# Graph network layer pair: 7 of 391 units of 256 edges fetched row by row from SyncE, GpSimd's ring cut from twelve units to ten

## The reference

```python
# layer 1: x = x + attention(relu(layernorm(x)))      (the change leaves it as it is)
# layer 2: h = relu(layernorm(x)); twice:
def _gcn_layer(x, W, b, src, dst, n_nodes):
    h = x @ W
    deg = segment_sum(ones, dst) + 2.0
    dinv = rsqrt(deg)
    msgs = h[src] * (dinv[src] * dinv[dst])[:, None]
    agg = segment_sum(msgs, dst, num_segments=n_nodes)
    return agg + h * (2.0 * dinv * dinv)[:, None] + b
```

## Time and profile before

| | us |
|---|---|
| median of three runs (4146.49 to 4154.21) | 4146.84 |
| profiled execution, span from first to last instruction | 4150.1 |
| first convolution, first to last gather issue | 1943.4 to 2919.7 |
| second convolution, first to last gather issue | 3132.6 to 4114.3 |
| busy: PE, DVE, ACT, POOL | 3489.9, 2288.9, 1798.3, 2607.4 |

### The profile page before, as it was taken

The page is one execution under the profiler, slowest core; times in us unless marked ns, Lnnn a source line. Parts: engine busy times, 40 slices in busy tenths (PEclk is TensorE's granted clock), DMA queues, the critical chain, the costliest instruction groups (busy, mean ns, idle before and its releaser), DMA issues.

```text
span 4150.1 us, 55488 instructions
## 1 busy us (share of the span) xinstructions
PE 3489.9 (84%) x15160; PEld 1694.2 (41%) x15160; DVE 2288.9 (55%) x3880; ACT 1798.3 (43%) x4172; POOL 2607.4 (63%) x2733
## 2 busy tenths in 40 slices
PE   5899988677888888898788888888997788888887
PEld 4499963222233333343333333333443333333332
DVE  6599887677777888885222333333552222333336
ACT  4356522444545555454333443444343333344442
POOL 3654411677777777654777777777106777777775
PEclk9999999899999999999999999999998999999999
DMA  7822325577777777665777777777216777777779
GB/s 285 244 67 61 90 76 208 172 210 210 210 210 211 210 210 211 190 206 190 210 210 210 210 210 210 211 210 210 79 66 211 211 210 210 210 210 210 210 209 351
DMA packets 318375, 804.24 MB, mean 194 GB/s; under 512 B 72905, under 2 KB 98139, under 8 KB 317129
## 3 DMA queue, kind: packets, MB, share of 16 engines
q0 software_dynamic: 199680, 630.72, 52.6%
q1 hardware_dynamic: 88925, 116.91, 8.5%
q10 hardware_dynamic: 29580, 54.49, 3.8%
HBM read 714.52 MB, written 88.21 MB: 193 GB/s over the span
## 4 chain that ended last, share of the span: by engine, by line
PE 34%; POOL 23%; issue 21%; DMA 12%; DVE 6%; SPq 1%; POOLq 1%; DVEq 1%; ACT 1%; ACTq 0%
POOL edge L1280 17%; PE mm L1529 8%; POOL rows_wmat L1280 5%; DMA edge<-h_tab,src_group 5%; DMA rows_wmat<-v_tab,src_group 4%; PE mm L1621 4%; PE sm L1693 4%; PE tr L1621 4%; PE mm L1693 4%; PE sm L1566 3%; PE tr L1693 2%; DVE edge L866 2%; PE tr L1524 1%; DMA ht_tab<-rows_wmat 1%; PE hist_ps L1693 1%
## 5 line engine op out<-in xcount | busy, mean ns | idle before, releaser
L1280 POOL DMA_INDIRECT edge<-h_tab,src_group x1564 | 1484.2, 949 | 708.5 <-issue 447.5
L1436 ACT ACTIVATE hots<-iota,drel 128x128 f32<-128x128 f32 x1760 | 538.0, 388 | 1174.5 <-PE tr L1693 606.9
L1280 POOL DMA_INDIRECT rows_wmat<-v_tab,src_group x782 | 739.4, 945 | 289.2 <-issue 272.4
L1693 PE MATMUL mm<-edge,hots 128*128 x880 | 465.9, 679 | 195.3 <-SPq L1098 189.7
L1693 PE MATMUL sm<-edge,hots 128*128 x880 | 442.6, 650 | 150.5 <-SPq L1098 148.1
L891 DVE TENSOR_TENSOR big<-big,mm 128x512 f32 x220 | 151.4, 688 | 686.6 <-PE tr L1693 668.8
L891 DVE TENSOR_TENSOR big<-big,sm 128x512 f32 x220 | 151.4, 688 | 602.6 <-PE misc L1693 588.6
L1693 PE MATMUL tr<-edge,hots 128*128 x880 | 395.6, 592 | 0.0
L1693 PEld LDWEIGHTS mm<-edge,hots 128*128 128x128 f32 x880 | 183.6, 217 | 470.1 <-issue 469.9
L1529 PE MATMUL mm<-rows_wmat 128*128 128x512 f32 x784 | 356.0, 598 | 0.0
L1693 PEld LDWEIGHTS sm<-edge,hots 128*128 128x128 f32 x880 | 175.8, 207 | 410.3 <-issue 410.0
(11 more groups left out here) (252 smaller groups left out, 4574.0 us busy)
## 6 DMA issues: line engine op xcount, KB each, us to landing
h_tab<-rows_wmat SPq DMA_DIRECT2D x98, 256.0 KB, 2.0
edge<-h_tab,src_group POOLq DMA_INDIRECT x1564, 3.7
rows_wmat<-low_tab SPq DMA_DIRECT2D x157, 128.0 KB
ht_tab<-rows_wmat SPq DMA_DIRECT2D x49, 256.0 KB
big<-ht_tab ACTq DMA_DIRECT2D x49, 256.0 KB, 2.8
v_tab<-rows_wmat ACTq DMA_DIRECT2D x49, 256.0 KB
x_tab<-big SPq DMA_DIRECT2D x49, 256.0 KB, 2.1
rows_wmat<-v_tab,src_group POOLq DMA_INDIRECT x782, 3.7
```

What stands on the lines that cost most here:

```text
L1280: pool.indirect_dma_start(ring[:, 2 * u + c, :], None, tab, bass.IndirectOffsetOnAxis(ap=src_group[:, n:n + 1], axis=0)).then_inc(a["rows_ ...
L1436: act.activation(group_hots[:, q % 2, e, :], iota[:, :], ACT.Abs, bias=drel[:, col:col + 1], scale=-1.0).then_inc(a["dist_set"], 1)
L1693: last = pe.matmul(agg_ps[bank][:, :], group_hots[:, q % 2, w % GROUP * 2 + n, :], edge[:, ds(slot[w % OFFS] + n * D, D)], start=(n == 0), ...
```

## The change

In each of the two convolutions, units 48, 97, 146, 195, 244, 293 and 342 (every 49th) are no longer gathered by GpSimd. SP fetches their 256 rows one by one, with 256 DMAs of 2 KB, whose source address comes from a register. The registers are read from a row of 256 offsets in SBUF, 16 at a time; that row is loaded by one DMA per unit from a new table, `offs_tab` (the sources times 512, made by one DVE operation on 128x782 integers and stored by SP before `low_tab`). These units lie in two slots of their own, at the place of the last two of the twelve; GpSimd's ring has the other ten.

SP does this inside its counting loop: it goes over the 192 pairs of units that GpSimd gathers, in seven rounds of 24 pairs and a last one of 24 without fetches. Ahead of the count of a pair it issues a batch of 16 rows, in two of every three pairs (BATCHES); at the end of a round it waits for the 256 rows and counts the unit. The attention layer keeps its ring of six, and its rows are counted as before. On DVE, the five operations that gave each step's slot in a ring of twelve become seventeen that give it in a ring of ten or in one of the two own slots; the rest of `gather` does the same wait and the same two indirect DMAs per unit.

```diff
-TWELFTH = -(-2 ** 16 // 12)
+EVERY = 49
+OWN = [g for g in range(UNITS) if g % EVERY == EVERY - 1]
+POOLED = [g for g in range(UNITS) if g % EVERY != EVERY - 1]
+POOL_SLOTS = RING[1] - 2
+BATCH = 16
+BATCHES = (1, 1, 0) * 8
...
+        own_offs = eler_hots[0:1, 0:2 * GE].bitcast(I32).rearrange("p (b e) -> p b e", b=2)
...
+            did(dve.tensor_scalar(off_i, src_flat[:, 0:J], float(D), None, ALU.mult))
+            marks["offs"] = prep[0]
...
-            did(dve.tensor_scalar(slotcol_i[1][:, :], gidx[:, :], float(TWELFTH), None, ALU.mult))
...
+            did(dve.tensor_scalar(slotcol_i[1][:, :], gidx[:, :], float(PER_EVERY), None, ALU.mult))
...
             sp.wait_ge(dve_prep, marks["low_T"])
+            sp.dma_start(offs_tab.rearrange("g e -> (g e)").rearrange("(p j) -> p j", j=J), off_i).then_inc(offs_kept, 16)
...
+            def load_offs(k):
+                sp.dma_start(own_offs[:, k % 2, :], offs_tab[OWN[k]:OWN[k] + 1, :]).then_inc(offs_in[k % 2], 16)
+
+            def fetch_and_count_rows(a, tab):
+                again = a["turn"] - 1
+                flat = tab.rearrange("n d -> (n d)")
+                own_before = [again * len(range(b, len(OWN), 2)) for b in range(2)]
+                batch = 0
+                load_offs(0)
+                for i in range(len(POOLED) // 2):
+                    k, at = divmod(i, len(BATCHES))
+                    if k < len(OWN):
+                        b = k % 2
+                        fetched = own_before[b] + k // 2 + 1
+                        if at == 0:
+                            batch = 0
+                            if k + 1 < len(OWN):
+                                load_offs(k + 1)
+                            sp.wait_ge(offs_in[b], 16 * fetched)
+                        for _ in range(BATCHES[at]):
+                            _, offs = nc.values_load_multi_w_load_instructions(
+                                own_offs[:, b, batch * BATCH:(batch + 1) * BATCH], engines=(mybir.EngineType.SP,), min_val=0,
+                                max_val=(NP - 1) * D, skip_runtime_bounds_check_because="rows of the edges' sources")
+                            for n in range(BATCH):
+                                c, p = divmod(batch * BATCH + n, P)
+                                at_slot = 2 * (POOL_SLOTS + b) + c
+                                sp.dma_start(gcn_ring[p:p + 1, at_slot, :], flat[ds(offs[n], D)].rearrange(
+                                    "(a n) -> a n", a=1)).then_inc(own_in[b], 16)
+                            batch += 1
+                    u = i % len(a["rows_in"])
+                    sp.wait_ge(a["rows_in"][u], a["rows_before"][u] + 64 * (i // len(a["rows_in"]) + 1))
+                    sp.sem_inc(a["rows_ready"], 2)
+                    if k < len(OWN) and at == len(BATCHES) - 1:
+                        sp.wait_ge(own_in[b], 16 * GE * fetched)
+                        sp.sem_inc(a["rows_ready"], 1)
...
-            count_rows(agg[1])
+            all_kept(sp, mids[0]["kept"])
+            sp.wait_ge(offs_kept, 16)
+            fetch_and_count_rows(agg[1], h2_tab)
...
-            count_rows(agg[2])
+            fetch_and_count_rows(agg[2], h3_tab)
...
-                for g in range(UNITS):
-                    u, past = g % units, g - units
+                for m, g in enumerate(a["pooled"]):
+                    u = m % units
+                    if m >= units and m % a["told"] == 0:
+                        freed = a["pooled"][m - units + a["told"] - 1]
...
```

More of the change, by code:

```diff
@@ L303, in build @@
         step_of = part(CUT.blocks * P).bitcast(I32)
+        off_i = part(J).bitcast(I32)
         g_from = part(CUT.blocks ** 2 * P // 2).bitcast(BF16).rearrange("p (g n) -> p g n", n=CUT.blocks * P)
@@ L361, in build @@
         ht_kept, low_before = low_in, [16 * len(range(n, TILES, HT)) for n in range(HT)]
-        gcn_rows_in = [sem(f"gcn_rows_in{u}") for u in range(RING[1] // 2)]
+        gcn_rows_in = [sem(f"gcn_rows_in{u}") for u in range(POOL_SLOTS // 2)]
+        own_in = [sem("own_in0"), sem("own_in1")]
+        offs_kept, offs_in = sem("offs_kept"), [sem("offs_in0"), sem("offs_in1")]
         gat_rows_in = [sem(f"gat_rows_in{u}") for u in range(RING[0])]
@@ L365, in build @@
         for n, (name, c) in enumerate((("gat", 0), ("gcn1", 1), ("gcn2", 1))):
-            units = RING[c]
             agg.append(dict(
-                units=units, told=1 + c,
+                units=(RING[0], POOL_SLOTS)[c], told=1 + c, pooled=(range(UNITS), POOLED)[c], turn=n,
                 rows_in=(gat_rows_in, gcn_rows_in)[c],
-                rows_before=[32 * (n == 2) * sum(1 for g in range(UNITS) if g % units // 2 == u) for u in range(units // 2)]
-                if c else [0] * units,
+                rows_before=[64 * (n == 2) * len(range(u, len(POOLED) // 2, POOL_SLOTS // 2)) for u in range(POOL_SLOTS // 2)]
+                if c else [0] * RING[0],
                 rows_ready=sem(f"{name}_rows_ready"),
@@ L658, in _ @@
             did(dve.tensor_scalar(slotcol_i[0][:, :], cols[:, 5, :], -1.0, float(2 * AW), ALU.add, ALU.mult))
[L659 removed]
+            turn_of, is_own, place, own_place = cols[:, 2, :], cols[:, 3, :], cols[:, 4, :], cols[:, 5, :]
+            did(dve.tensor_scalar(slotcol_i[1][:, :], gidx[:, :], float(PER_EVERY), None, ALU.mult))
             did(dve.tensor_scalar(slotcol_i[1][:, :], slotcol_i[1][:, :], 16, None, ALU.arith_shift_right))
[L661 to L663 removed]
+            did(dve.tensor_copy(turn_of, slotcol_i[1][:, :]))
+            issue(dve.scalar_tensor_tensor(is_own, turn_of, -float(EVERY), cols[:, 0, :], ALU.mult, ALU.add))
+            issue(dve.tensor_tensor(place, cols[:, 0, :], turn_of, ALU.subtract))
+            did(dve.tensor_scalar(slotcol_i[1][:, :], slotcol_i[1][:, :], 1, None, ALU.bitwise_and))
+            issue(dve.tensor_scalar(is_own, is_own, float(EVERY), None, ALU.is_ge))
+            did(dve.tensor_copy(own_place, slotcol_i[1][:, :]))
+            issue(dve.tensor_scalar(own_place, own_place, float(POOL_SLOTS + 1), None, ALU.add))
+            did(dve.tensor_scalar(slotcol_i[1][:, :], place, -1.0, float(PER_POOL), ALU.add, ALU.mult))
+            did(dve.tensor_scalar(slotcol_i[1][:, :], slotcol_i[1][:, :], 16, None, ALU.arith_shift_right))
+            did(dve.tensor_copy(turn_of, slotcol_i[1][:, :]))
+            did(dve.scalar_tensor_tensor(place, turn_of, -float(POOL_SLOTS), place, ALU.mult, ALU.add))
+            did(dve.tensor_tensor(own_place, own_place, place, ALU.subtract))
+            did(dve.tensor_tensor(own_place, own_place, is_own, ALU.mult))
+            did(dve.tensor_tensor(place, place, own_place, ALU.add))
+            did(dve.tensor_scalar(slotcol_i[1][:, :], place, -1.0, float(2 * D), ALU.add, ALU.mult))
             did(dve.tensor_tensor(cols[:, 4, :], cols[:, 1, :], stepf[:, 0:blocks], ALU.add))
@@ L1093, in count_rows @@
             def count_rows(a):
[L1095 to L1098, removed]
+                for g in range(UNITS):
+                    u = g % a["units"]
+                    sp.wait_ge(a["rows_in"][u], 32 * (g // a["units"] + 1))
+                    sp.sem_inc(a["rows_ready"], 1)
@@ L1265, in gather @@
             def gather(tab, a, ring, done):
-                units, ends = a["units"], None
-                for g in range(UNITS):
-                    u, past = g % units, g - units
-                    if past >= 0:
-                        if past % ENDS == 0:
+                units, ends, held = a["units"], None, -1
+                for m, g in enumerate(a["pooled"]):
+                    u = m % units
+                    if m >= units and m % a["told"] == 0:
+                        freed = a["pooled"][m - units + a["told"] - 1]
+                        if freed // ENDS != held:
+                            held = freed // ENDS
                             _, ends = nc.values_load_multi_w_load_instructions(
-                                ends_row[:, past:min(past + ENDS, UNITS - units)], engines=(mybir.EngineType.Pool,),
+                                ends_row[:, held * ENDS:min((held + 1) * ENDS, UNITS)], engines=(mybir.EngineType.Pool,),
                                 min_val=1, max_val=SP, skip_runtime_bounds_check_because="clamped when the table is made")
-                        if past % a["told"] == 0:
-                            freed = min(past % ENDS + a["told"], len(ends)) - 1
-                            wait_alone("pool", pool, done, ends[freed] & WORD)
+                        wait_alone("pool", pool, done, ends[freed % ENDS] & WORD)
                     for c in range(2):
```

4 lines of the change are left out of this document (added).

## The result

The changed kernel takes 4231.98 us (median of four runs, 4222.93 to 4252.03) against 4146.66 for the kernel before; the ratio is 1.0211, with a 95% interval of 1.0185 to 1.0237. 4248 was forecast, in a range of 4112 to 4340. The profiled execution has a span of 4230.6 us, 80.5 more than before.

What follows compares the result with a forecast made beforehand. GpSimd's gather descriptors were taken as the bound, 2.50 us a unit. Added were 90 us for both convolutions, 7 for SP's late start and 4 early: 101 on 4150.1 gives 4251, less 3.3 for the median, 4248 us; range 4112 to 4340.

Steps and rivals of the forecast that it cites:

- the late start: Second convolution: 12 loads keep SP for 7.2 us while GpSimd already gathers; 7 us more where SP sets the pace.
- The round: SP's work for one own unit and 24 pairs: 129.4 us, against 120.1 for GpSimd.
- GpSimd's stalls: Gaps before GpSimd's gathers, ended by PE's matmuls, as its ring fills: some 60 us per convolution.
- some 20 us of lateness: How late SP must be before GpSimd stands in its wait on the ring of ten.
- A row: SP's cost to fetch one row, address instructions and issue together: 0.43 us.
- the break-even: Price per row on SP at which a layer is as long as before: 0.405 us.
- a register load: SP loading 16 row offsets into registers: 1.06 us plus 0.04 of gap, 1.10, sixteen times a round.
- Rival (a): SP keeps up through a cheaper row, GpSimd stays the bound: full 35 us gain less 4, 4116 us; chance 0.27.
- The last 48 units: End of each convolution, gathered by GpSimd alone: 115 us, 120.1 less a lead of 5.
- The early part: Longer slot-table chain on DVE, offsets product and SP's store before the gathers: 4 us more, between 0 and 8.
- (c): Issuing a row on SP costs as much as 128 rows, 0.53 to 0.55 us: 4600 to 4680 us; chance 0.07.
- (d): DMA engines hold SP up, a unit's rows all on one engine: about 5050 us at the higher price; chance 0.06.

Runs made afterwards that it cites:

- bytes: Changed kernel with row offsets stored and transfers declared as bytes, so SP needs no multiplication per row; 4133.01 us, ratio 0.9958.
- even55_early: Changed kernel with every 55th unit on SP, rows spread over 26 of 27 pairs, second convolution's first offsets loaded before its x1 loads; 4124.43 us.
- early: Changed kernel with the second convolution's first offsets loaded ahead of the twelve x1 loads; 4226.89 us, ratio 1.0194.
- bytes_early: Changed kernel with offsets in bytes and the second convolution's first offsets loaded ahead of the twelve x1 loads; 4124.45 us, ratio 0.9949.
- even: Changed kernel with a round's 256 rows spread over 23 of 24 pairs, 11 or 12 in each; 4231.31 us, ratio 1.0203.
- best47: Changed kernel with byte offsets, evenly spread rows, early offsets, a later wait for SP's own unit, and every 47th unit on SP; 4109.87 us.

## Why the prediction was right

The mechanism holds: SP becomes the pace, GpSimd stalls on its ring, and the loss lies in the two stretches alone, +40.5 and +42.0 against 45 and, with the late start, 52. Of the 101 us forecast the profiled execution has 80.5. By its steps:

- **The round.** 129.4 us were forecast; the first 672 gathers, seven rounds, take 2840.2 - 1942.2 = 898.0, or 128.3 each. GpSimd's stalls (gaps over the usual 0.30), forecast at some 60 us a convolution, sum to 58 in each. They begin sooner than forecast: some 20 us of lateness, at 9 us a round, would have taken two rounds, and the first wait comes 26 us after the first gather. The sum is not touched by that, since it counts SP's rounds.
- **Its terms were off in both directions.** A row takes 0.392 us from start to start (0.43 forecast): the address costs an ALU_OP of 0.033, not a FUSED_REGOPS of 0.043, and the issue 0.227, not 0.246. That median alone would have put SP below the break-even of 0.405. Against it stand terms that the sum lacked: a register load costs 1.157 + 0.03 (1.10 forecast, 1.4 us a round); SP pauses for 0.35 us about every 43 rows (2.2 us a round, below), and with the pauses and some longer steps the mean row of the first convolution is 0.405; and SP waits 3.5 us a round, 1.4 of it for its own last rows to land, which the sum left out. SP's own work is 124.8 us a round in the first convolution and 123.0 in the second, still over GpSimd's 120.1. So the size of the round was right by luck: its errors cancelled, and with the median row alone the sign would have been the other one.
- **Which side it falls on.** Rival (a)'s condition, one instruction less, is what "bytes" does (the ALU_OP goes and not the MOVE), and it changes the sign. The time that rival gave, 4116, was too low even with the late start repaired (4124.45). The Trainium skill, DMA: Bandwidth & Descriptors, section on issuing engines not being separate DMA queues, says that issuing from several engines only saves the sequencer's time to start a DMA, and that this time is usually small beside the DMA. The first half agrees with even55_early, where 1792 issues on SP spare GpSimd 2.50 us a unit. The second half is no guide here. A row leaves two packets, by the DMA view of 2100 to 2840:

```profile
q1 hardware_dynamic: 2961, 3.03, 1.5%
...
edge<-h_tab SPq DMA_DIRECT2D x1480, 2.0 KB
```

  These two take the DMA engines some 0.12 us together (an estimate: 1.5% of 16 engines in 740 us, over 2961 packets), less than the issue's 0.227; and it is SP's side, down to the 0.033 for a row's address, that decides the sign.
- **The late start.** +7 us were forecast in the second convolution. SP's first row is later than that, 17.6 us after the first gather where it is 5.9 in the first convolution: the load of offsets stands behind the 12 loads, and SP waits 9.9 us for it to land. SP's timeline (start, time spent issuing) and its waits show it:

```profile
3172.24 5.90 SPq L1241 DMA_DIRECT2D rows_wmat<-x_tab  x12
3178.18 0.63 SPq L1128 DMA_DIRECT2D eler_hots<-offs_tab  x2
...
SPq L1148 <- DMA eler_hots<-offs_tab: 9.9, 1, 9.9
```

  Yet the second convolution loses hardly more than the first, 42.0 against 40.5. A term that the sum did not have offsets the late start: the issue of a row takes 0.220 us there, in the first convolution 0.228, which is 14 us over 1792 rows. In "early" both go the other way: the start is repaired, and the issue takes 0.225. So the start is late as forecast, and more so, but no run shows what it costs by itself while SP sets the pace. Where GpSimd is the pace, its stretch is 12 us longer with the late start ("bytes" against "bytes_early").
- **The last 48 units.** 115 us were forecast, from a lead of 5. They take 120.1 in the first convolution and 127.0 in the second, where the last 97 gathers are longer in the kernel before too (mean 1000 ns there, 1019 after).
- **The early part.** +4 us were forecast, and nothing was measured: the first gather starts at 1942.2 against 1943.4, although the product for the offsets takes 0.571 us and the store is there.
- **Rivals (c) and (d).** (c) falls by the issue, 0.227 in the median and 0.292 at most; (d), though its two packets a row are there, by gathers that land as before, and by even55_early, whose 1792 rows a convolution slow no gather.

What stays open: how SP's waits on gathers arise, some 2 us a round (3.5 less 1.4). They hang on the bunching, since in "even" they go while GpSimd's stalls stay as long (55 us against 58). It is open too why the issue of a row differs by some ns between convolutions and kernels. And in even55_early 4.8 us of the gain are lost between the last gather of the first convolution and the first of the second (217.7 us against 212.9); no run here followed that.

## What to carry to other kernels

When work moves from a bottleneck engine to an idle one, compare both engines round by round, not by their totals: the price on the new engine is all that its queue does per item (address arithmetic, register loads, waits for its own transfers), and a few per cent of capacity decide the sign. Then look at what else that engine does for others: here a count that releases TensorE stands in line behind the rows, so rows are better spread evenly where the round has slack, and the first load better issued ahead of bulk loads. Search the number of items moved: here the eighth unit still paid, and the ninth, with which the new engine was full, cost more than it saved.

## What the runs showed of the hardware

- **A pause in SP's straight code.** The records of SP's instructions show a gap of 0.35 us after every 128 of them (between 2100 and 2300 us at the 163rd, 291st, 419th, and so on), where the median gap is 0.04. The DMA queue of kind "instruction", q14, moves more when SP issues rows, as the DMA view of 2100 to 2840 shows, before and after:

```profile
q14 instruction: 20, 0.16, 0.1%
```

```profile
q14 instruction: 55, 0.45, 0.2%
```

  In 740 us that is 35 packets of 8.2 KB more; SP's 1480 rows of three instructions each in the same window are 4440, or 34.7 times 128, and there are 37 such pauses. In "bytes", with two instructions a row, it is 45 packets. The Trainium skill, Runtime: NRT & Kernel Launch, section Instruction fetch mechanics, says that the sequencer fetches its code by a DMA queue of its own, in blocks of 16 KiB or 256 instructions, and that crossing one is mostly hidden. The packets agree with the first; the size differs, 128 instructions and 8.2 KB here, and on SP it isn't hidden. That the pause is this fetch is argued from the counts, not shown by a run of its own.
- **The granted clock of TensorE** is, in the mean, 0.90 in the stretches that SP paces, 0.94 before, 0.94 to 0.95 in best47, and 0.97 in the last 48 units. It goes between two levels, 2.4 GHz (1.00) and 1.2 (0.50): the stretch at 0.50 shown above lies in its wait of 8.46 us for SP's count and in the first matmuls behind it; until 1985, with matmuls one behind the other, it had been at 1.00. TensorE's busy time over a convolution hardly changes (810 us against 812).
- **The issue of a DMA of one row of 2 KB** takes SP 0.220, 0.225 or 0.228 us in the median of a convolution's 1792 rows, by convolution and kernel (second of the changed kernel, second of "early", first of the changed kernel). No run shows what sets it.
- **A load of 16 registers** takes 1.157 us on SP, where GpSimd's took 1.06; 1.237 in "even", where loads and rows alternate with the counts.
